# Merging the table and projection stages of a transformer kernel, and requesting the first attention operands inside them

## What is computed

```python
q = (x @ Wq.T + bq).reshape(B, T, H, hd)      # B=2, T=2048, H=16 heads of hd=16
k = (x @ Wk.T + bk).reshape(B, T, H, hd)
v = (x @ Wv.T + bv).reshape(B, T, H, hd)
scores = jnp.einsum('bqhd,bkhd->bhqk', q, k) * hd ** -0.5
decay = jnp.exp(-alpha * jnp.abs(idx[:, None] - idx[None, :]))
attn = jax.nn.softmax(scores * decay, axis=-1)
out = jnp.einsum('bhqk,bkhd->bqhd', attn, v)
# then Wo, layer norm, an FP4 feed-forward, linear attention,
# a mixture of 8 experts, each with a layer norm after it
```

## Time and profile before

| | |
|---|---|
| median of 3 runs | 3701.16 us (3688.95 to 3708.16) |
| profiled execution, its own time | 3675.41 us |
| span in the profile | 3673.5 us |
| mean granted TensorE clock | 0.912 |
| first DMA of `stage_tables` issued | 17.86 us |
| last DVE instruction of `stage_project` ends | 213.1 us |
| first matmul of `stage_attention` | 273.13 us |

### The profile page before, as it was taken

One profiled execution on the slowest core, in us unless ns is written; L12 is line 12 of the kernel. 1 busy time (PEld: TensorE's weight loads), 2 busy tenths in 40 slices (PEclk: granted clock), 3 DMA queues, 4 the chain that ended last, 5 costly groups with the idle time before them and its releaser, 6 DMA issues. The chain is left out here.

```text
span 3673.5 us, 67142 instructions
## 1 busy us (share of the span) xinstructions
PE 3074.7 (84%) x22724; PEld 1712.2 (47%) x22725; DVE 2534.7 (69%) x6796; ACT 1738.0 (47%) x2072; POOL 1442.3 (39%) x746
## 2 busy tenths in 40 slices
PE   3619999999999999999844378877999996999992
PEld 1301333333333333333313344445666665999992
DVE  5739999999999999999426767773555554333335
ACT  2300788888888888888951112221222221111114
POOL 2320777787877778787840000000001002111110
PEclk8855999999999999999976689998999997999996
DMA  2842333433343433333013100003000004555554
GB/s 76 226 147 54 83 86 86 86 86 86 86 86 86 86 85 84 85 81 79 29 27 62 34 18 18 11 1 107 13 13 25 13 13 137 183 185 178 181 185 156
DMA packets 197621, 308.66 MB, mean 84 GB/s; under 512 B 86224, under 2 KB 142384, under 8 KB 195184
## 3 DMA queue, kind: packets, MB, share of 16 engines
q1 hardware_dynamic: 188576, 282.09, 29.7%
q0 software_dynamic: 7632, 22.16, 1.7%
q10 hardware_dynamic: 1152, 1.05, 0.1%
HBM read 238.91 MB, written 62.13 MB: 82 GB/s over the span
## 5 line engine op out<-in xcount | busy, mean ns | idle before, releaser
L702 DVE CUSTOM_DVE_ANT_0 ps_r<-ps_r,toep 128x512 f32<-128x512 f32 x2048 | 1352.6, 716 | 130.5 <-PE ps_r L635 89.9
L791 ACT ACTIVATE prob<-ps_s,csc 128x1024 f32<-128x1024 f32 x768 | 830.6, 1119 | 141.6 <-PE ps_s L657 119.8
L635 PE MATMUL ps_r<-p 96*128 96x512 bf16 x2048 | 740.9, 400 | 87.2 <-DMA p<-scr_scratch 73.3
L749 POOL TENSOR_TENSOR tb<-tb,toep 128x1024 f32<-128x1024 f32 x256 | 605.7, 2366 | 410.0 <-ACT tb L781 353.7
L657 PE MATMUL ps_s<-p 120*128 120x512 bf16 (+1 forms) x2048 | 611.7, 381 | 33.3 <-ACT tb L781 24.8
L752 POOL TENSOR_TENSOR tb<-tb,mb 128x1024 f32<-128x1024 f32 x256 | 605.4, 2365 | 20.1
L673 PE MATMUL ps_o<-prob,vp 128*32 128x256 f32 x8192 | 549.8, 386 | 1.9 <-ACT prob L788 1.5
L635 PEld LDWEIGHTS ps_r<-p 96*128 96x128 bf16 x2048 | 197.9, 97 | 560.4 <-DVE mp L702 340.4
L781 ACT ACTIVATE tb<-ps_s 128x1024 f32<-128x1024 f32 x256 | 263.4, 1029 | 174.0 <-PE ps_s L657 172.5
L673 PEld LDWEIGHTS ps_o<-prob,vp 128*32 128x32 f32 x8192 | 214.3, 109 | 270.4 <-issue 178.0
L657 PEld LDWEIGHTS ps_s<-p 120*128 120x128 bf16 (+1 forms) x2048 | 189.4, 98 | 246.7 <-ACT tb L781 63.8
(11 more groups left out here) (295 smaller groups left out, 3229.1 us busy)
## 6 DMA issues: line engine op xcount, KB each, us to landing
moe_w<-in_W_dram SPq DMA_DIRECT2D x79, 1024.0 KB, 5.3
p<-scr_scratch SPq DMA_DIRECT2D x288, 192.0 KB
mb<-mrow_scratch SPq DMA_DIRECT2D x16, 2048.0 KB, 8.7
scr_scratch<-part SPq DMA_DIRECT2D x64, 384.0 KB, 6.0
p<-scr_scratch SPq DMA_DIRECT2D x96, 128.0 KB
moe_pt<-slots_scratch SPq DMA_DIRECT2D x72, 132.0 KB, 2.1
vscr_scratch<-vsb SPq DMA_DIRECT2D x2, 4096.0 KB, 15.6
vp<-vscr_scratch SPq DMA_DIRECT2D x16, 512.0 KB, 22.7
```

The costliest lines, as they stand in the source:

```text
L635: pe.matmul(ps_r[:, bank, :], buf[:, hh, 0, qt * P:(qt + 1) * P], buf[:, hh, 1, kc * CH:(kc + 1) * CH], start=True, stop=True)\
L702: dve.tensor_tensor_reduce(ps_r[:, bank, :], ps_r[:, bank, :], toep[:, col:col + CH], 1.0, -3.0e38, ALU.mult, ALU.max, mp[:, whose.par, hh ...
L749: pool.tensor_tensor(tb[:, k % DIAGS], tb[:, k % DIAGS], toep[:, col:col + CH].unsqueeze(1) .broadcast_to([P, 2, CH]), ALU.mult).then_inc( ...
L791: act.activation(prob[:, n % RING], ps_s[:, mine % 2], ACT.Exp, scale=csc[:, qb * TB + kb:qb * TB + kb + 1]).then_inc(s["exp"], 1)
```

## The change

`open_sems` shares the clearing among the five engines. `stage_tables` and `stage_project` become one block, `stage_prologue`. It takes 4 pieces of `SUPER` = 1024 columns, and in each of them four units u (two `jt`, each two chunks of 512). `part` has 1024 columns for each `jt`, `full` and `rest` have two buffers, `vsb` holds one piece, and so SP stores v once for each piece. The middle cast moves from DVE to ACT and stands there after the high casts of the next unit. `LEFT` of each batch's first chunk and `RIGHT` of its last are not made. The clearing of `p2[0]` (POOL, in unit 1), the load of `w6` into it, and the first `load_p1`, `load_p2`, `load_p1` stand in the new block. The matching work for `p2[1]` stands at the head of the attention block.

```diff
     with nc.Block() as block:
         @block.gpsimd
         def _(pool):
-            for mine in s.values():
-                for n, sem in mine.items():
-                    pool.sem_clear(sem)
+            clear(pool, 0)      # and vector 1, scalar 2, tensor 3, sync 4 of flat[share::5]
...
+SUPER = 2 * CH
+SUPERS = B * T // SUPER
+def parts_of(u):
+    chunk = (2 * (u // 4) + u % 2) % QB
+    return [RAW, KEY] + ([LEFT] if chunk else []) + ([RIGHT] if chunk < QB - 1 else [])
...
+            # sync
+                sp.wait_ge(s["cev"], up_to(1))
+                for r, e in enumerate(K_PARTS):
+                    sp.dma_start(g["w6"][r].rearrange("q (t p) -> (q t) p", p=P), wt[:, e, :]).then_inc(s["loaded"], 16)
+                sp.wait_ge(s["loaded"], up_to(48 + 16 * 6))
...
+                for sc in range(SUPERS):
+                    b, half = divmod(sc, SUPERS // B)
+                    for jt in range(2):
+                        sp.wait_ge(s["low"], up_to(parts_upto(4 * sc + 2 * jt + 2)))
+                        for i in range(4):
+                            dst = g["scr"][b * HP + 4 * jt + i, :, :, :, half * SUPER:(half + 1) * SUPER]
+                            sp.dma_start(dst.rearrange("v e d t -> d (v e) t"),
+                                         part[32 * i:32 * i + 32, jt].rearrange("d v e t -> d (v e) t")).then_inc(s[f"out{jt}"], 16)
+                        if sc == 2 and jt == 0:
+                            for k in range(2):
+                                sp.wait_ge(s[f"out{k}"], up_to(2 * 64))
+                            load_p1(sp, Pair(0, 0))
+                        if sc == 2 and jt == 1:
+                            load_p2(sp, Pair(0, 0))
+                        if sc == 3 and jt == 0:
+                            load_p1(sp, Pair(0, 1))
+                    sp.wait_ge(s["v_ev"], up_to((sc + 1) * 2 * TPC))
+                    sp.dma_start(g["vscr"][...], vsb[:]...).then_inc(s["vout"], 16)
...
+            # scalar, in each unit u
+                    if sc and par == 0:
+                        act.wait_ge(s[f"out{jt}"], up_to(sc * 64))
+                    for i, var in enumerate(parts_of(u)):
+                        ...                                      # high cast
+                    if u:
+                        middle(u - 1)                            # waits rest of u - 1
...
+            # gpsimd
+                load_x(0)
+                load_x(1)
+                # iotas: c4, grow, toep; ident; memset of part[LEFT, 0:CH]
+                    if u == 1:
+                        pool.wait_ge(s["scaled"], up_to(scaled_upto(1)))
+                        pool.memset(p2[0][ROWS:ROWS + AUG, :, LEFT:RIGHT + 1, :], 0.0).then_inc(sa["setup"], 1)
...
+            # vector, in each unit u
+                    if u == 2:
+                        dve.wait_ge(s["ctr"], up_to(1))
+                        dve.tensor_copy(wt[:], ps_t[:]).then_inc(s["cev"], 1)
+                    ...                                          # rest(u)
+                    if u:
+                        low(u - 1)                               # waits mid of u - 1
+                    if u % 2:
+                        values(2 * sc + jt)
+                # in values(chunk):
+                    if sc and par == 0:
+                        dve.wait_ge(s["vout"], up_to(16 * sc))
...
-                        load_p1(nxt)
-                        load_p1(nxt.plus(1))
-                        load_p2(nxt)
                         load_v(nxt)
+                        for hh in range(2):
+                            sp.dma_start(p2[1][ROWS:ROWS + AUG, hh, KEY, :],
+                                         g["w6"].rearrange("r q t -> (r q) t")).then_inc(s["waug"], 16)
```

More of the change, by code:

```diff
@@ L64, in open_sems, with clear @@
     s = {stage: {n: ctx.enter_context(nc.semaphore(stage + n)) for n in names.split()} for stage, names in SEMS.items()}
+    flat = [(n, sem) for mine in s.values() for n, sem in mine.items()]
+    def clear(eng, share):
+        for n, sem in flat[share::5]:
+            eng.sem_clear(sem)
+            if n not in FROM_ZERO:
+                eng.sem_inc(sem, 1)
     with nc.Block() as block:
@@ L78, in up_to @@
     return n + 1
[L81 to L160, removed]
-                sp.dma_start(g["bq"][:], a["bq"].rearrange("(c p) -> p c", p=P), allow_slow_non_contiguous=True).then_inc(s["loaded"], 16)
-                sp.dma_start(g["bk"][:], a["bk"].rearrange("(c p) -> p c", p=P), allow_slow_non_contiguous=True).then_inc(s["loaded"], 16)
-                sp.wait_ge(s["cev"], up_to(1))
-                for r, part in enumerate(K_PARTS):
-                    sp.dma_start(g["w6"][r].rearrange("q (t p) -> (q t) p", p=P),
-                                 wt[:, part, :]).then_inc(s["wstored"], 16)
-                sp.wait_ge(s["wstored"], up_to(16 * 6))
@@ L468, in ring_use, with parts_upto, scaled_upto, pair_loads @@
     return out
-def stage_attention(nc, g, a):
+SUPER = 2 * CH
[3 more added lines that the diff above has]
+    return [RAW, KEY] + ([LEFT] if chunk else []) + ([RIGHT] if chunk < QB - 1 else [])
+def parts_upto(u):
+    return sum(len(parts_of(n)) for n in range(u))
+def scaled_upto(u):
+    return parts_upto(u) - 2 * u
+def pair_loads(g, s, p1, p2):
+    def load(sp, dst, var, into, j, sem):
+        for r, n in RUNS:
+            first = 0 if var == KEY else Q_PARTS[r]
+            for hh in range(2):
+                src = g["scr"][j.c:j.c + 1, var, first:first + (n if var == KEY else 1),
+                               hh * HD:(hh + 1) * HD].rearrange("a e d t -> (a e) d t")
+                if var != KEY and n > 1:
+                    src = src.broadcast_to([n, HD, T])
+                sp.dma_start(dst[HD * r:HD * (r + n), hh, into, :], src).then_inc(sem, 16)
+    def load_p1(sp, j):
+        for into, var in enumerate((RAW, KEY)):
+            load(sp, p1[j.par], var, into, j, s[f"p1load{j.par}"])
+    def load_p2(sp, j):
+        for hh in range(2):
+            for r, part in enumerate(Q_PARTS):
+                src = g["scr"][j.c:j.c + 1, RAW:RIGHT + 1, part, hh * HD:(hh + 1) * HD, :]
+                sp.dma_start(p2[j.par][HD * r:HD * r + HD, hh, RAW:RIGHT + 1, :],
+                             src.rearrange("a v d t -> d (a v) t")).then_inc(s[f"p2load{j.par}"], 16)
+        load(sp, p2[j.par], KEY, KEY, j, s[f"p2load{j.par}"])
+    return load_p1, load_p2
@@ L490, in stage_attention @@
         toep, csc, ident = g["toep"], g["csc"], g["ident"]
[L492 to L510 removed]
+        load_p1, load_p2 = pair_loads(g, s, p1, p2)
         def walk(body):
@@ L741, in body @@
                     if this is None:
+                        pool.memset(p2[1][ROWS:ROWS + AUG, :, LEFT:RIGHT + 1, :], 0.0).then_inc(s["setup"], 1)
                         return
```

390 lines of the change are left out of this document (218 added, 172 removed).

## The result

| | median, us | runs | ratio to before, 95% interval |
|---|---|---|---|
| before | 3691.07 | 20 (3658.86 to 3708.16) | |
| after | 3699.14 | 20 (3688.62 to 3711.5) | 1.0046 (1.0028 to 1.0064) |

The forecast was 3705 with a range of 3672 to 3728, and "within 0.5%" as the likeliest case. The time is in the range. The change makes the kernel slower by 0.5%, and the ratio lies at the edge of that case. The moment on which the forecast stands was missed by 19.6 us all the same, as the profile shows: its span is 3696.3 us, its own time 3698.01.

A forecast was written before the change was run, and what follows sets the result against it. Attention's first matmul was taken to set the time: 22.0 us removed up to the first store, 66.6 added to block's end, 39.7 removed behind; + 4 after rounding on 3675.4, plus 25.8 to the median, gave 3705, range 3672 to 3728.

The forecast's parts named there:

- within 0.5%: Whole kernel: the time stays within 0.5% of before; likeliest case, chance 0.60.
- The moment on which the forecast stands: Start of attention's first matmul, forecast at 278 us against 273.1 before; a microsecond there is one of the total.
- The start: From kernel opening to first store group: leaves at 44.3 us against 66.3 before, 13.4 of the saving being clears.
- The price of a group: Transfer of one 3.15 MB store group in the merged block: 13.0 us, or 14.9 to landing.
- the 1.9 around it: Time around a store group's transfer, split from the 9.3 us measured before, with 7.4 for the transfer.
- the middle two: Among four group transfer estimates, 7.7 to 17.2 us: 12.4 (twice the 16-partition rate) and 14.8 (old 7.4 doubled).
- the slower rival: Store groups keep the pace inside one DMA, 17.2 us each: + 25 us, 3730; chance 0.18.
- The loop: Between groups: group k waits for k - 1 to land, every second one for the v store; 47 us a piece.
- The loads inside: From group 4 on, loads share SP's in-order queue with stores: 72 us of loads, block ending at 277.5.
- the second rival: Stores overtake the loads in the queue, block ends at 221.2, 56 us less: 3649; chance 0.06.
- From the profile to the median: Step from the forecast profiled time, 3679, to the median, 3705: 25.8 us added, as in the runs shown before.
- slower by over 0.5%: Whole kernel: more than 0.5% (18.5 us) slower than before; chance 0.18.

The follow-up runs named there:

- experiment 10: Changed kernel with POOL's clear of `p2[0]` moved from unit 1 ahead of its first product; median 3690.44 us, ratio to before 0.9995.
- experiments 3 to 5: Changed kernel with v store ahead of each piece's second group; middle casts and low parts ahead of waits; both: 3675.25, 3678.43, 3643.71 us.
- experiment 9: Changed kernel with every load cut into DMAs of 16 partitions; median 3669.42 us, ratio to before 0.9945.
- clears only: Kernel before, with only the 157 semaphore clears shared among five engines; median 3681.45 us, ratio to before 0.9979.

## Why the prediction was right, and where it was not

The mechanisms ahead of attention were all there, three of their sizes were wrong, and that the time was met is in large part luck: the first matmul was forecast 19.6 us too early, and the way from there to the median 25.5 us too long. The terms, as forecast and as measured:

| term | forecast | measured |
|---|---|---|
| first store group leaves | 44.3 | 48.83 |
| group's issue to ACT's cast | 14.9 | 17.8 (66.64 - 48.83) |
| from the cast to the next issue | 6.2 | 5.66 (72.30 - 66.64) |
| second group's issue to the v store landed | 20.9 | 22.95 (95.25 - 72.30) |
| v landed to the next issue | 6.1 | 5.66 (100.91 - 95.25) |
| groups 0 to 4 | 94.9 | 103.1 |
| group 4 to the v store landed | 80.3 | 79.4 (231.31 - 151.93) |
| group 6 to the first matmul | 52.4 | 60.65 (297.61 - 236.96) |

**The start, + 4.5.** 1.6 of it is the opening (first DMA at 5.98, forecast 4.4). Most of the rest of ACT's delay comes from the 2.77 us operation of DVE, which took 2.57 more than in the kernel before. That POOL's clear in unit 1 holds ACT's casts was in the working, and experiment 10 confirms it; moving it gave 4.5. That the same clear costs DVE nothing held for the operations that ran beside it there: five subtractions of DVE (`rest`, TENSOR_TENSOR) between 28.0 and 32.0 took 0.63 to 0.65 us each, as at 37.7 in experiment 10, where POOL does nothing.

**The price of a group.** I took 13.0, "between the middle two". It was 15.9 (17.8 less the 1.9 around it), and 3.15 MB at 197 GB/s are 16.0. The term that was mis-sized is that choice: 13.0 us is 242 GB/s, near the 246 of two stores that meet, and that happens for 2 us in 16. Twice the rate of 16 partitions, 254 GB/s, was too high as well. Up to group 4 that is + 2.9 and + 2.7 for two landings and + 2.05 twice for the v stores, less 1.5 for the shorter way from landing to issue: + 8.2. At the first matmul the slower rival was nearer than the forecast: its cause was there (195 GB/s for its 183), its bound of 15.4 us was passed, and its + 25 stands beside + 19.6 measured, of which, however, the start and the last stretch have 12.8. Only the median kept the forecast right, below.

**The loop.** Two waits in series, a period alternating with `jt`, group k held by the landing of group k - 1: right, and experiments 3 to 5 show that each is real and that together they give at least their sum (25.5 + 21.0 against 50.4).

**The loads inside.** One queue in order, three engines of 16: right to within a microsecond for the stretch from group 4 to the v store (79.4 against 80.3), but as a sum of two errors: group 5 landed 51.0 us behind group 4's issue, where the working had 45.9, and the v store 28.3 behind that (202.94 to 231.28), where it had 34.4. The last stretch was 8.3 too short. I let the backlog of `load_p1` run off beside group 7 and gave the v store its 6 us at all 16 engines' rate. In the trace the last 12 us have 0.13 of the engines busy, as much as two of 16, and group 7's last store and the v store end with them; with the loads spread (experiment 9) this tail is gone. The stage ends with its slowest DMA engine, and a sum of mean rates has no term for that. (The Trainium skill, DMA: Bandwidth & Descriptors, section Why a DMA increments its semaphore by 16 and not by 1, lets the engine count of a DMA follow from its shape; the trace agrees in kind, 0.19 of the engines busy in the changed kernel and 0.66 with 16 partitions to a DMA.) Loads hidden by overtaking, the second rival, did not occur: group 5 landed 26.0 us after its issue (176.93 to 202.94), and the v store behind the loads waited too.

**From the profile to the median.** I added 25.8 us, the distance between the profiled run of before (3675.41) and the median of three. Of this 10.1 was the three runs, whose median of 3701.16 lies above that of all twenty, 3691.07. The other 15.7 was the profile, a fast one. The changed kernel's profiled run lies 1.1 below its median (3698.01, 3699.14). With the first matmul at 297.6 my own working would have said 3725: still in the range, but a case of its own, slower by over 0.5%.

From one profiled run to the other the time grows by 22.6 us (3675.41 to 3698.01) where the first matmul moves by 24.5, so the tail of the program is the same to 2 us, as forecast. But the runs of before fall into two clusters, 3659 to 3678 and 3686 to 3708. The runs of before that were made beside the experiments do too, and in all of them the mean granted clock is 0.912 to 0.918 in the lower cluster and 0.899 to 0.907 in the upper one. One place where such differences arise is the linear attention, hundreds of us behind the change. Its busy time by stretch, first before, then clears only, then after (first column behind the stretch: its length; the clock is third from the end):

```profile
2493.00:3060.00 567.00, 516.31 (x5227) 358.30 (x5227) 304.48 (x893) 152.04 (x280) 55.89 (x58) 0.95 0.09 29
```

```profile
2472.00:3073.00 601.00, 552.69 (x5227) 382.37 (x5227) 305.53 (x893) 151.88 (x279) 56.01 (x58) 0.86 0.08 28
```

```profile
2498.00:3083.00 585.00, 534.18 (x5227) 369.67 (x5227) 305.70 (x896) 152.50 (x280) 56.02 (x58) 0.90 0.09 28
```

The same 5227 matmuls take 567 to 601 us at a mean granted clock from 0.95 down to 0.86. So a single profile of this kernel can be off by up to 34 us from here. It is not the only place: the changed kernel's profile is 18 us longer here than before's and makes up for it in the stages ahead. What decides the clock in a given run is open: no experiment was aimed at it. Open is also why the runs of no merged version fall into two clusters so far apart.

**What the change was worth in parts.** By the first matmul: clears shared, 8.9 us earlier in the kernel before. Merging on top, with the loads left outside: 4.0 later. Loads inside: 29.4 later. So the early loads cost more than the rest gave. By the medians the version with the loads outside is faster than before (0.9956), by more than its 4.9 us at the first matmul: the median less the first matmul is 3418 and 3417 us for before and clears only, and about 3400 for the merged versions. For the changed kernel this is 16 us, and they offset most of the 24.5 that it loses at the first matmul. They lie behind the change. The attention stage has little of them: from its first matmul to the first DMA of the stage behind it, it takes 1672 us before (273.13 to 1945.37) and 1668 after (297.61 to 1965.72). Where the rest arises is not shown. So the cost of the change is 23 us by the two profiled runs and 8 by the medians, and the runs do not say whether the difference belongs to the change.

## What to carry to other kernels

Price a transfer by what its partitions can move and by how many engines its shape lets it use, and then ask which transfers of the same queue stand behind it: a load that is early in time but on 3 of 16 engines holds back every store after it. In a loop with a store in it, put everything that completes the next store ahead of the wait for the last one, and split stores over two queues so that both halves of the partitions are busy. When a forecast is one handover plus a tail that does not change, take the tail from many runs, not from one profile and three.

## What the runs showed of the hardware that was not expected

- A DVE TENSOR_SCALAR of 128x64 float32 took 2.77 us instead of 0.20 while POOL cleared a tile (13.51 to 16.16), and ended with it. Another took 5.22 beside the clear of `p2[0]` (clear early), and one of 128x2 took 2.36 beside POOL's iota of `toep`. So an operation of POOL that only writes can hold DVE up. It does not hold every operation: TENSOR_TENSOR beside the clear of `p2[0]` in the changed kernel kept its 0.63 to 0.65 us. Which property of the instruction decides was not tested.
- In one queue four stores of 32 adjacent partitions each move at 195 to 197 GB/s; half of them on a second queue makes it 385, with the DMA engines about as busy in both cases (0.95 to 0.97, and 1.05).
- Twelve loads that kept 0.19 of the DMA engines busy held the stores queued behind them. The same bytes in DMAs of 16 partitions brought the first matmul 29.6 us forward.
- Halving the pieces from 2 KB to 1 KB cost a store 5% of its rate (188 against 197 GB/s).
